# First group's channel attention moved into the last merged turn and the second cross attention, 26 of its expert chunks beside the second half's feed-forward and projections, and seven chunks a turn in place of nine

## The chip, the cores and the metric

The kernel runs on one core of one Trainium2 chip. The metric is the device time of one execution in microseconds; the median of several runs counts. The core's engines are TensorE (PE, with its weight loads PEld), VectorE (DVE), ScalarE (ACT), GpSimd (POOL) and SyncE (SP), which here only issues DMAs. They run their own instruction lists in written order and wait for each other by semaphores.

## The reference, cut to what matters

A decoder with two layers over x of 16 sequences × 128 tokens × 128 channels, in f32. Layer 0: four encoder layers of linear attention with 16 heads and a feed-forward; cross attention against a context with 16 heads and a mask; a feed-forward with quantized weights and activations, in which a depthwise convolution over three tokens stands between the two products. Layer 1:

```python
# self attention with 16 heads of 8, each row keeps its 64 largest scores
# channel attention (_L1_xattn), n = 128 tokens, 4 heads of d = 32 channels, with global and local weights
scores = jnp.einsum('bhdn,bhen->bhde', qh, kh) * scale
attn = jax.nn.softmax(scores, axis=-1)
out = jnp.einsum('bhde,bhen->bhdn', attn, vh)
# mixture of 8 experts, all of them over all tokens (HIDDEN 128, FFN 512)
y = sum over experts of (silu(h @ Wg) * (h @ Wu)) @ Wd
```

Every step has a residual sum, and most have a layer norm in front.

## The kernel before, in words

The 16 sequences are two halves of 8; a half is two slots (s = 0, 1) of G = 4 sequences, and a slot of a half is a group (g = 0 to 3) in layer 1. A tile of a slot is 128 × 512 f32. PSUM has eight banks of 128 × 512.

The program is, on each engine: `encode_half` (half 0 through the encoder), `cross_and_forward(0)`, `beside_encoder` (half 0's topk self attention, sequence by sequence, merged with half 1's encoder: the merged turns, b = −1 to 9), `cross_and_forward(1)`, and then one loop over points `t`. Twelve points are one turn, which belongs to one sequence b of the topk attention: at turn b the signs and penalties of b are worked on, the search for the 64th largest score of b−1, and the probabilities and outputs of b−2. The loop begins at `START2` = 84, turn 7, and the topk part ends with turn 17, at point 216. There is no run-time planner: each engine's order is what these point lists say, and a function `topk(b, p, half)`, `channel(g, r)`, `expert_chunk(k)`, `gate(k)` or `hidden(k)` issues on each engine what belongs to the point.

`channel(g, r)` is the channel attention of group g, r = 0 to 11, from point `CH_START[g]` on: keys with their row weights on GpSimd (r 0 and 2), statistics and normalization (r 1, 2), queries (r 3, 4), 64 small score matmuls (r 5), softmax (r 6, 7), spreading of the weights into blocks on GpSimd (r 7), output matmuls (r 8), residual, statistics and normalization again (r 9, 10), and a transpose into `hTm`, the experts' input (r 11). It goes through PSUM bank 3. It starts at 84 (group 0), 102 (group 1), 166 and 214.

An expert chunk k is one of 4 pieces (128 hidden channels) of one of 8 experts for one group: 32 a group, 128 in all. TensorE makes the gate product into bank 5 or 6 (line 1519), the down product of chunk k−3 into bank 4 (1509), and the up product into bank 3 or 7 (1528); ScalarE applies Silu (1045); VectorE multiplies (2008). `chunk_points` places the chunks: from 12 points behind their group's `CH_START`, at the points `CHUNK_PTS` of a turn (nine of twelve), and behind point 216 at every point. So turns 8 to 17 have nine each, and 38 come in the tail. SyncE loads an expert's three 256 KB weights into one of two buffers when the chunks of the one before last are done.

In `cross_and_forward(hf)`, the core of the cross attention runs eight iterations (one a sequence): scores into banks 0 to 3; on VectorE a masked copy (2277), row maxima (2282), sums of the iteration before (1752), and the folding of heads for the outputs of three iterations back (1761, 1764); exponentials on ScalarE; subtraction and scaling on GpSimd; transposes through banks 4 and 5, outputs (1225) into banks 6 and 7 by turns. Then come the quantized feed-forward, c = 0 to 3 with two slots each, slot 0 in banks 0 to 3 and slot 1 in 4 to 7, the second quantization and product, a layer norm and the projections for the topk attention.

Of the kernel before, what the change touches and what calls it, by code (L numbers as in the profile page):

```python
# [26 lines left out]
P = 128  # L27
NSEQ = 16
SLOTS = 2
G = 4  # L30
# [51 lines left out]
CROSS_BANKS = (((2, 3, 0, 1), (6, 7, 4, 5)), ((3, 4, 5, 5), (6, 7, 4, 5)))  # L82

# [36 lines left out]

def gate_point(t):

    return t + max(0, 2 - t % PTS) if t < TURNS * PTS else t


def hidden_point(t):
    return t if t >= TURNS * PTS else t + 2 if t % PTS < 2 else t + 1
# [28 lines left out]
U_BANK, U_PREV = u_banks()  # L156

# [13 lines left out]
def decoder(nc, x, ctx, mask, aw, acolA, acolB, arow, w2a, bw, bcol, brow, cw, cconv, dw, dcol, drow,  # L171
            erow, ecol, mg, mu, md, ident_d, const_d, pos_d, out):
    stack = ExitStack()
    with stack:
# [142 lines left out]
        def flat(t):  # L317
# [5 lines left out]
                   [t[:, :, :].rearrange("p b c -> p (b c)")[:, 0:2 * P].bitcast(BF16).rearrange("p (i q) -> p i q", i=4) for t in xin]]  # L323
# [4 lines left out]
        hid = [big[1][:, i, :] for i in range(CH)]  # L328
        hp = h[0]
        hTm = [hT[1][:, :], flat(xb[1])]  # L330
        sg = [qe[s][:, :] for s in range(SLOTS)]
        ctxp = ctxt[0]
        ctxTp = cbuf[0][:, :, 1:P + 1]
        ysb = ctxt[1]
        chq, chk = kk, ke
        chv = [xb[0], h[1]]
        ablk = [t[:, :, 0:P] for t in vv]
# [98 lines left out]
        def _(sp):  # L436
# [72 lines left out]
            def load_keys(g):  # L509
                sp.dma_start(ctxp[:, :, :], cv[:, g * G:(g + 1) * G, :]).then_inc(ctxp_in, 16)  # L510

            for l in range(L - 1):
# [10 lines left out]
                load_down(l + 1)  # L523
            sp.wait_ge(at_mm, 2)
# [3 lines left out]
            load_keys(0)  # L528
            for e in range(2, NG * NEXP):
                if e % NEXP == 2 and e // NEXP + 1 < NG:  # L530
# [12 lines left out]
        def _(pool):  # L543
# [35 lines left out]
            def core_cross(hf):  # L579
# [30 lines left out]
                for b in range(1, NB):  # L610
# [5 lines left out]
                    if b + 2 < NB:  # L616
                        spread(b + 2)

# [20 lines left out]
            def spread_queries(b):  # L639
                g, c = b // G, b % G  # L640
                if b >= 2:
                    pool.wait_ge(st_mm, 2 * (b - 2) + 2)
                pool.tensor_tensor(qblk[b % 2],
# [56 lines left out]
            def channel(g, r):  # L700
                x = xs_of[g // SLOTS][g % SLOTS]
                if r == 0:
# [5 lines left out]
                    for k in range(2):  # L708
                        pool.tensor_tensor(chk[k][:, :, :], ctxp[:, :, :], bc(rowe[:, 4 + 2 * k, :]), ALU.mult).then_inc(c_k, 1)
# [9 lines left out]
                if r == 7:  # L719
# [3 lines left out]
                    for k in range(2):  # L723
                        pool.tensor_tensor(ablk[k].rearrange("p a (q e) -> p a q e", q=EH),
# [48 lines left out]
            def beside_encoder():  # L773
# [3 lines left out]
                for b in range(-1, NB + 2):  # L777
                    merged_turn(b)
                    if b == NB:
                        for s in SL:  # L780
                            ln_rsqrt(s, NLN + LN_B)

# [43 lines left out]
            for t in range(START2, LAST_POINT):  # L826
                if t < TURNS * PTS:
                    topk(t // PTS, t % PTS, 1)
                for g in range(NG):
# [3 lines left out]
        def _(act):  # L833
# [29 lines left out]
            def core_cross(hf):  # L863
                for b in range(NB + 2):
                    if 1 <= b <= NB:
                        exponentials_by_head(hf, b - 1)
                    if b >= 2:
                        copy_probs(hf, b - 2)

            def projected(s, hf):  # L870
                qT, kT = qT_of[hf], kT_of[hf]

                hT_copy(s, hf * NTR + TR_D, 4 * s)
                act.wait_ge(pk_mm, nth(s, hf * 2 + 2))
                act.activation(kT[s][:, :], bank(4 * s + 2), ACT.Identity, bias=catt[1][:, 1:2]).then_inc(pk_done, 1)
                act.wait_ge(pq_mm, nth(s, hf * 2 + 2))
                act.activation(qT[s][:, :], bank(4 * s + 1), ACT.Identity, bias=catt[1][:, 0:1]).then_inc(pq_done, 1)
# [8 lines left out]
            def signs(n, heads):  # L886
# [3 lines left out]
                if n >= 2:  # L890
                    act.wait_ge(z_ready, 3 * n - 3)
                for hd in heads:
# [114 lines left out]
            def beside_encoder():  # L1007
                for b in range(-1, NB + 2):
# [3 lines left out]
                    if b == NB + 1:  # L1012
                        context_queries(1)
                        attended_out(1, 6)

            def channel(g, r):
                if r == 0 and g > 1:
                    attended_out(g, 3)
                if r == 2:
                    act.wait_ge(cT_mm, g + 1)  # L1020
                    act.copy(ctxTp, bank4(3)).then_inc(cT_out, 1)
                if r == 3:
# [5 lines left out]
                    if g == 0:  # L1028
                        act.wait_ge(base_done, 4 * HALVES)
                    for k in range(2):  # L1030
                        act.activation(chv[k][:, :, :], ctxTp, ACT.Identity, bias=cole[:, 2 * k + 1:2 * k + 2], scale=cole[:, 2 * k:2 * k + 1]).then_inc(c_v, 1)
# [3 lines left out]
                if r == 11:  # L1035
                    act.wait_ge(m_mm, g + 1)
                    if g >= 2:
                        act.wait_ge(u_mm, NCHUNK * (g - 1))
                    act.copy(hTm[g % 2], bank(3)).then_inc(m_out, 1)  # L1039
# [1443 lines left out]
```

## Time and profile before

| | |
|---|---|
| median of 3 runs | 1509.03 us (1507.82 to 1510.85) |
| the profiled execution, its own time | 1503.95 us |
| its span | 1502.0 us |
| mean granted TensorE clock, share of full | 0.805 |
| busy: PE, PEld | 1055.0, 626.8 us |
| busy: DVE, ACT, POOL | 989.8, 663.2, 484.4 us |
| moved by DMAs | 41.22 MB, mean 27 GB/s |

The page gives busy time per engine, then 40 slices of the span (37.6 us each), in which a digit is the busy share in tenths. The clock row is in tenths of full speed, 2.4 GHz; TensorE is granted 2.4 or 1.2 GHz, and values between are means. Ends of matmuls are modelled, and they overlap, so what one costs is read from the distance of starts. A timeline gives instructions in order of time, with equal neighbours merged, and in square brackets the idle time of the engine before it and what ended it.

### The profile page before, as it was taken

The numbers are of one execution on the slowest core, as the hardware profiler recorded it, in microseconds if no ns is written. First come the engines' busy times: TensorE is split into PE (matmuls) and PEld (weight loads), VectorE is DVE, ScalarE is ACT, GpSimd is POOL, SyncE is SP. The second block draws the span as 40 slices with busy tenths as digits, with TensorE's granted clock in tenths as the row PEclk, the third lists the DMA queues.
The fourth block names the chain that finished last, engine by engine and source line by source line (L and its number), as shares of the span: only waits on it lengthen the run. The fifth ranks groups of instructions, "written<-read, shape, count | busy, mean of one in ns | idle before, by whom it ended". The sixth has DMA issues, their size and how long they took to land. (4 is left out here: it accounts for less than half of the span.)

```text
span 1502.0 us, 16867 instructions
## 1 busy us (share of the span) xinstructions
PE 1055.0 (70%) x4698; PEld 626.8 (42%) x4698; DVE 989.8 (66%) x3078; ACT 663.2 (44%) x1751; POOL 484.4 (32%) x446
## 2 busy tenths in 40 slices
PE   3877745545667277787655545769999487998798
PEld 2766622323445155565433323334444144453333
DVE  6566678887467877775858887376666776644222
ACT  2444427532566255563127433455666255323121
POOL 4233337403345144443227305442222143101000
PEclk9899967855677577775558756799999778999899
DMA  3110010000000000000010000011211001112111
GB/s 120 29 28 19 18 47 1 1 0 1 1 13 17 13 17 13 17 2 1 1 49 1 1 0 8 1 42 43 64 57 43 21 22 42 57 63 63 49 63 49
DMA packets 34124, 41.22 MB, mean 27 GB/s; under 512 B 5280, under 2 KB 19248, under 8 KB 34032
## 3 DMA queue, kind: packets, MB, share of 16 engines
q1 hardware_dynamic: 33360, 38.21, 8.2%
q0 software_dynamic: 672, 1.98, 0.4%
q8 instruction: 34, 0.56, 0.2%
q14 instruction: 58, 0.48, 0.1%
HBM read 39.13 MB, written 1.05 MB: 27 GB/s over the span
## 5 line engine op out<-in xcount | busy, mean ns | idle before, releaser
L2008 DVE TENSOR_TENSOR big<-psum,qe 128x512 f32<-128x512 f32 x128 | 87.7, 687 | 211.6 <-PE psum L1528 103.7
L1045 ACT ACTIVATE qe<-psum 128x512 f32<-128x512 f32 x128 | 75.1, 596 | 199.0 <-PE psum L1519 196.5
L1509 PE MATMUL psum<-big,wexp 128*128 128x512 f32 x256 | 135.3, 612 | 0.0
L903 ACT ACTIVATE far<-far,half_far,fmul 128x128 bf16<-128x128 bf16 x256 | 103.2, 487 | 51.7 <-DVE hit L1786 51.7
L1799 DVE MAX8 near<-Wk 128x8 f32<-128x128 f32 x512 | 103.5, 276 | 1.2 <-DVE Wk L1809 0.2
L572 POOL TENSOR_SCALAR veps<-mv 128x4 f32<-128x4 f32 x34 | 8.3, 246 | 276.2 <-DVE mv L1706 276.2
L1148 PE MATMUL psum<-ident,h 128*128 128x128 f32 x176 | 38.5, 350 | 79.8 <-DVE h L1713 48.0
L661 POOL TENSOR_TENSOR Wk<-Wk,far 128x1024 f32<-128x1024 f32 x32 | 69.2, 2162 | 73.2 <-ACT far L903 73.2
L1284 PE MATMUL psum<-ctxT,kT 32*128 32x512 f32 x128 | 46.2, 802 | 55.5 <-DVEq L1875 42.0
L1528 PE MATMUL psum<-hT,wexp 128*128 128x512 f32 x128 | 70.6, 634 | 20.7 <-DVE big L2008 20.7
L1713 DVE TENSOR_SCALAR h<-xs,mv,rstd 128x128 f32<-128x128 f32 x128 | 56.5, 504 | 41.9 <-POOL rstd L574 38.7
L1214 PE MATMUL psum<-ident,Wk 128*128 128x128 f32 x256 | 47.1, 351 | 45.1 <-POOL Wk L615 41.4
L1519 PE MATMUL psum<-xb,wexp 128*128 128x512 f32 x128 | 72.7, 652 | 8.4 <-DMA wexp<-in_md 7.1
L1509 PEld LDWEIGHTS psum<-big,wexp 128*128 128x128 f32 x256 | 50.7, 198 | 65.1 <-issue 64.9
L1519 PE MATMUL psum<-hT,wexp 128*128 128x512 f32 x128 | 72.8, 652 | 4.6 <-DMA wexp<-in_md 3.6
L893 ACT ACTIVATE far<-S 128x128 bf16<-128x128 f32 x256 | 75.2, 297 | 0.3
L883 ACT ACTIVATE S<-psum,tiny 128x1024 f32<-128x1024 f32 x32 | 35.6, 1114 | 84.6 <-PE psum L1266 84.6
L1528 PE MATMUL psum<-xb,wexp 128*128 128x512 f32 x128 | 67.6, 611 | 6.8 <-DVE big L2008 6.8
L652 POOL TENSOR_TENSOR Wk<-S,ngr 128x2048 f32<-128x2048 f32 x16 | 57.8, 3609 | 44.3 <-DVE hit L1786 44.3
L1809 DVE MATCH_REPLACE8 Wk<-near,Wk 128x128 f32<-128x128 f32 x256 | 67.3, 276 | 0.0
L1148 PEld LDWEIGHTS psum<-ident,h 128*128 128x128 f32 x176 | 25.8, 178 | 95.0 <-DVE h L1713 43.7
L1214 PEld LDWEIGHTS psum<-ident,Wk 128*128 128x128 f32 x256 | 37.4, 180 | 66.2 <-POOL Wk L615 40.5
(320 smaller groups left out, 2705.9 us busy)
## 6 DMA issues: line engine op xcount, KB each, us to landing
wexp<-in_mg SPq DMA_DIRECT2D x32, 256.0 KB, 2.7
wexp<-in_mu SPq DMA_DIRECT2D x32, 256.0 KB, 3.0
wexp<-in_md SPq DMA_DIRECT2D x32, 256.0 KB, 3.5
w<-in_aw SPq DMA_DIRECT2D x8, 256.0 KB, 2.8
w<-in_w2a SPq DMA_DIRECT2D x8, 256.0 KB, 2.6
ctxt<-in_ctx SPq DMA_DIRECT2D x8, 256.0 KB, 4.2
wqkv<-in_aw SPq DMA_DIRECT2D x8, 192.0 KB, 2.2
xin<-in_x SPq DMA_DIRECT2D x4, 256.0 KB, 3.2
```

The lines of the kernel that those rows point to most:

```text
L661: pool.tensor_tensor(Wk[t][:, heads, :], Wk[t][:, heads, :], far[t][:, heads, :], ALU.subtract).then_inc(z_ready, 1)
L893: ins = act.activation(far[n % 2][:, hd, :], S[n % 3][:, hd, :], ACT.Sign, accum_out=cnt[n % 2][:, hd:hd + 1])
L903: ins = act.activation(far[t][:, hd, :], far[t][:, hd, :], ACT.Identity, bias=half_far[:, 0:1], scale=fmul[t][:, hd:hd + 1])
L1045: act.activation(sg[k % 2], bank(5 + k % 2), ACT.Silu).then_inc(silu_done, 1)
L1148: mm = pe.transpose(dst[:, b * P:(b + 1) * P], src[:, b, :], eye)
L1214: mm = pe.transpose(bank(4 + g % 2)[:, j * P:(j + 1) * P], E[a % 2][:, 4 * g + j, :], ident[:, :])
L1509: pe.matmul(bank(4), wd[e % 2][:, c, :], hid[k % CH], start=(k % NCHUNK == 0), stop=(k % NCHUNK == NCHUNK - 1), skip_group_check=True).the ...
L1519: pe.matmul(bank(5 + k % 2), wg[e % 2][:, c * P:(c + 1) * P], hTm[g % 2], start=True, stop=True).then_inc(g_mm, 1)
L1528: pe.matmul(bank(U_BANK[k]), wu[e % 2][:, c * P:(c + 1) * P], hTm[g % 2], start=True, stop=True).then_inc(u_mm, 1)
L1799: ins = dve.max(near[:, hd, rank:rank + 8], Wk[t][:, hd, :])
L1809: ins = dve.match_replace(Wk[t][:, hd, :], near[:, hd, 0:8], Wk[t][:, hd, :], TAKEN)
L2008: dve.tensor_tensor(hid[k % CH], bank(U_BANK[k]), sg[k % 2], ALU.mult).then_inc(hu_done, 1)
```

## The change

Group 0's channel attention and its first 26 expert chunks get points below 84: `FIRST` = 46 is the first. A function `beside(n)` on each engine issues the next n points of them. It is called with 2 points in the last merged turn, with 4, 3 and 3 behind cross-attention iterations 1 to 3 of the second half, and with 26 in the second half's feed-forward and projections: two behind the first product, three in each of the four convolution steps, four around the second product, and four behind each slot's projections. Group 1's channel attention starts at 84 in place of 102. `CHUNK_PTS` has seven points in place of nine, and point 1 of a turn is left out beside a channel attention. To make room, the second half's feed-forward and projections use banks 0 to 3 alone (two a slot), its cross attention's outputs use bank 6 alone, group 0's channel attention and all early up products use bank 7, and several tiles are placed elsewhere.

```diff
-CH_START = (START2, START2 + 18, (2 * G + 5) * PTS + 10 + (G - 4) * PTS, (3 * G + 5) * PTS + 10 + (G - 4) * PTS)
+PRE_TURN, PRE_CROSS, PRE_FORWARD = 2, (4, 3, 3), 26
+FIRST = START2 - PRE_TURN - sum(PRE_CROSS) - PRE_FORWARD
+CH_START = (FIRST, START2, (2 * G + 5) * PTS + 10 + (G - 4) * PTS, (3 * G + 5) * PTS + 10 + (G - 4) * PTS)
-CHUNK_PTS = (0, 1, 3, 4, 5, 6, 7, 9, 10)
+CHUNK_PTS = (0, 1, 3, 4, 6, 7, 9)
...
+OUT_BANKS = ((6, 7), (6, 6))
+FORWARD_BANKS = (((0, 1, 2, 3, 0, 1, 2), (4, 5, 6, 7, 4, 5, 6)), ((0, 1, 0, 1, 0, 1, 0), (2, 3, 2, 3, 2, 3, 2)))
+PROJECT_BANKS = (((0, 2, 1, 3), (4, 6, 5, 7)), ((0, 1, 0, 1), (2, 3, 2, 3)))
+CROSS_OUT_BANKS = ((2, 3), (0, 3))
+X_BANK = (7, 3, 3, 3)
...
-            while t < TURNS * PTS and t % PTS not in CHUNK_PTS:
+            while START2 <= t < TURNS * PTS and (t % PTS not in CHUNK_PTS or t % PTS == 1 and any(c <= t < c + X_FREE for c in CH_START)):
...
-        q = 7 if in_x(t) or k % 2 else 3
+        q = 7 if t < START2 or in_x(t) or k % 2 else 3
...
+            point = [FIRST]
+            def beside(n):                     # TensorE's; the other engines' are alike
+                for _ in range(n):
+                    channel(0, point[0] - CH_START[0])
+                    for k in CHUNKS_OF.get(point[0], ()):
+                        expert_chunk(k)
+                    point[0] += 1
...
@@ TensorE, cross attention: outputs(a) @@
-                    if a >= 2:
+                    if a >= 1 and hf == 1:
+                        pe.wait_ge(o_done, n)
+                    elif a >= 2:
                         pe.wait_ge(o_done, n - 1)
...
@@ TensorE, feed-forward @@
                 first(0)
+                if hf == 1:
+                    beside(2)
                 for c in range(CH):
                     if c + 1 < CH:
                         first(c + 1)
                     for s in SL:
+                        if hf == 1:
+                            beside(1)
                         pe.wait_ge(c_conv, nth(s, hf * CH + c + 1))
...
+                    if hf == 1:
+                        beside(1)
...
                 for s in SL:
                     topk_projections(s, hf)
+                    if hf == 1:
+                        beside(4)
...
@@ SyncE: the first group's context is loaded earlier, the second's with a wait @@
+            sp.wait_ge(q_pos, both(1, 2 * L))
+            load_keys(0)
             sp.wait_ge(at_mm, 2)
             for k in range(2):
                 load_expert(k, k)
             sp.wait_ge(ctxT_mm, nth(1, HALVES))
-            load_keys(0)
+            sp.wait_ge(c_k, 2)
+            sp.wait_ge(cT_mm, 1)
+            load_keys(1)
```

## Rows read from the trace of the kernel before

**Rows 1.** The page: busy time by engine, and 40 slices of PE and of its clock.
```profile
PE 1055.0 (70%) x4698; PEld 626.8 (42%) x4698; DVE 989.8 (66%) x3078; ACT 663.2 (44%) x1751; POOL 484.4 (32%) x446
...
PE   3877745545667277787655545769999487998798
...
PEclk9899967855677577775558756799999778999899
```
**Rows 2.** Windows: length, busy us (x) of PE PEld DVE ACT POOL, clock, DMA share, GB/s.
```profile
769.00:851.00 82.00, 44.09 (x250) 23.22 (x250) 69.64 (x59) 49.90 (x167) 46.18 (x21) 0.73 0.05 17
851.00:872.00 21.00, 8.19 (x38) 3.93 (x38) 14.78 (x52) 2.74 (x6) 2.53 (x4) 0.64 0.00 0
872.00:899.00 27.00, 11.53 (x43) 5.68 (x42) 25.47 (x43) 12.32 (x18) 0.00 (x0) 0.63 0.00 1
899.00:923.00 24.00, 17.32 (x96) 11.40 (x94) 19.70 (x59) 8.22 (x14) 11.64 (x11) 0.67 0.00 0
923.00:951.00 28.00, 9.76 (x97) 6.46 (x97) 15.61 (x44) 11.43 (x41) 10.45 (x12) 0.54 0.04 10
951.00:985.00 34.00, 29.35 (x126) 11.76 (x127) 14.94 (x27) 21.09 (x64) 17.65 (x16) 0.88 0.08 24
985.00:1028.00 43.00, 31.49 (x89) 14.18 (x90) 31.30 (x113) 23.52 (x70) 14.61 (x15) 0.92 0.12 38
...
1068.00:1106.00 38.00, 34.71 (x138) 17.33 (x137) 25.32 (x97) 24.55 (x69) 11.42 (x11) 1.00 0.21 66
1106.00:1143.00 37.00, 35.35 (x126) 16.79 (x126) 24.18 (x94) 23.57 (x67) 11.06 (x10) 0.95 0.14 43
1143.00:1204.00 61.00, 36.07 (x134) 17.78 (x134) 43.02 (x198) 24.39 (x68) 14.42 (x14) 0.84 0.08 26
1204.00:1258.00 54.00, 44.33 (x211) 23.98 (x208) 41.15 (x124) 29.22 (x74) 20.71 (x17) 0.83 0.10 34
1258.00:1303.00 45.00, 36.51 (x124) 18.77 (x121) 26.82 (x104) 17.77 (x35) 11.61 (x11) 0.89 0.18 60
1303.00:1336.00 33.00, 32.04 (x128) 16.14 (x126) 19.30 (x76) 11.47 (x16) 2.04 (x2) 1.00 0.15 48
1336.00:1370.00 34.00, 31.13 (x117) 16.15 (x116) 7.46 (x15) 9.19 (x14) 0.00 (x0) 1.00 0.15 47
1370.00:1401.00 31.00, 20.16 (x121) 9.72 (x120) 16.82 (x39) 8.83 (x13) 8.30 (x9) 0.92 0.16 52
1401.00:1502.00 101.00, 90.74 (x206) 38.67 (x205) 23.41 (x34) 20.28 (x34) 0.00 (x0) 0.97 0.18 60
```
**Rows 3.** Timeline of PE in the tail: start, us, first matmuls of two chunks running.
```profile
1408.79 1.02 PE L1519 MATMUL psum<-xb,wexp 128*128 128x512 f32 x2
...
1411.37 1.02 PE L1519 MATMUL psum<-xb,wexp 128*128 128x512 f32 x2
```
**Rows 4.** The page's groups: busy, mean ns of one; idle before, and releasers.
```profile
L2008 DVE TENSOR_TENSOR big<-psum,qe 128x512 f32<-128x512 f32 x128 | 87.7, 687 | 211.6 <-PE psum L1528 103.7
```
**Rows 5.** Timelines of PE and DVE in two cross-attention iterations, at half and full clock.
```profile
802.25 1.93 PE L1225 MATMUL psum<-big,vv 128*32 128x512 f32 x8 [0.68 <-ACT big L851]
804.11 1.90 PE L1202 MATMUL psum<-kblk,qT 32*128 32x512 f32 x8
...
813.10 1.06 PE L1225 MATMUL psum<-big,vv 128*32 128x512 f32 x8 [0.68 <-ACT big L851]
814.10 1.14 PE L1202 MATMUL psum<-kblk,qT 32*128 32x512 f32 x8
...
815.45 2.47 DVE L2277 COPY_PREDICATED S<-maskt,psum 128x2048 f32<-128x2048 int32 x1 [1.16 <-PE psum L1202]
```
**Rows 6.** Timeline of ACT in turn 12: a table load, the last chunk's gate.
```profile
1115.28 1.28 ACT L1045 ACT_TABLE_LOAD   x1
...
1139.43 0.60 ACT L1045 ACTIVATE qe<-psum 128x512 f32<-128x512 f32 x1 [1.98 <-PE psum L1519]
```
**Rows 7.** Timelines of POOL and DVE in turn 7's channel attention.
```profile
920.44 2.93 POOL L709 TENSOR_TENSOR ke<-ctxt,rowe 128x512 f32<-128x512 f32 x2
...
925.92 3.75 DVE L1940 TENSOR_SCALAR h<-xs,mv,rstd 128x128 f32<-128x128 f32 x4 [1.58 <-POOL rstd L698]
```

More of the change, by code:

```diff
@@ L156 @@
 U_BANK, U_PREV = u_banks()
+EARLY = sum(t < START2 for t in CHUNK_AT)
 def channels_by(t):
@@ L828, in _ @@
                     topk(t // PTS, t % PTS, 1)
-                for g in range(NG):
+                for g in range(1, NG):
                     channel(g, t - CH_START[g])
@@ L891, in signs @@
                     act.wait_ge(z_ready, 3 * n - 3)
+                if n == NB and heads[0] == 0:
+                    act.wait_ge(d_mm, EARLY)
                 for hd in heads:
@@ L1083, in encode_half, with beside @@
                                                bias=colB[:, 2 + c:3 + c]).then_inc(hid_done, 1)
+            point = [FIRST]
+            def beside(n):
+                for _ in range(n):
+                    channel(0, point[0] - CH_START[0])
+                    for k in GATES_OF.get(point[0], ()):
+                        gate(k)
+                    point[0] += 1
             def context_keys(hf):
@@ L1136, in _ @@
                     topk(t // PTS, t % PTS, 1)
-                for g in range(NG):
+                for g in range(1, NG):
                     channel(g, t - CH_START[g])
@@ L1252, in core_cross @@
                         scores(b + 1)
+                    if hf == 1 and 1 <= b <= len(PRE_CROSS):
+                        beside(PRE_CROSS[b - 1])
                 project_outputs(1)
@@ L1655, in cross_and_forward @@
                             pe.wait_ge(c_silu, nth(s, hf * CH + c))
-                        transposes(bank(4 * s + 3), yT[s], ident[:, :], c_yT_mm)
+                        transposes(bank(FORWARD_BANKS[hf][s][3]), yT[s], ident[:, :], c_yT_mm)
+                    if hf == 1:
+                        beside(1)
                 for s in SL:
@@ L1683, in _ @@
                     topk(t // PTS, t % PTS, 1)
-                for g in range(NG):
+                for g in range(1, NG):
                     channel(g, t - CH_START[g])
@@ L2013, in result, with beside @@
                 dve.tensor_tensor(x[:, :, :], bank4(3), x[:, :, :], ALU.add).then_inc(y_done, 1)
+            point = [FIRST]
+            def beside(n):
+                for _ in range(n):
+                    channel(0, point[0] - CH_START[0])
+                    for k in HIDDEN_OF.get(point[0], ()):
+                        hidden(k)
+                    point[0] += 1
             def act_scales(s, n):
@@ L2290, in cross_and_forward @@
                         cross_outputs(hf, b - 3)
+                    if hf == 1 and 1 <= b <= len(PRE_CROSS):
+                        beside(PRE_CROSS[b - 1])
                     if b == NB:
@@ L2325, in cross_and_forward @@
                 quantize(1)
+                if hf == 1:
+                    beside(2)
                 def chunk_max(s, c):
@@ L2409, in _ @@
                     topk(t // PTS, t % PTS, 1)
-                for g in range(NG):
+                for g in range(1, NG):
                     channel(g, t - CH_START[g])
```

175 lines of the change are left out of this document (113 added, 62 removed).

## The prediction

> **What bounds the kernel now.** I read the engines' shares and the 40 slices first. TensorE is busy 70% of the span, VectorE 66%, and neither is busy all the time: TensorE stands mostly at 4 to 7 tenths up to slice 26 and mostly at 8 to 9 from there on [rows 1]. So the second reading is a table of windows, one per stage of the last 730 us [rows 2]. The second half's cross attention is 769 to 851: VectorE 69.6 of 82 us. The convolutional feed-forward and the projections are 851 to 923; from 872 on VectorE works 45 of 51 us and TensorE 28.9 at a granted clock of 0.65. In turn 7 (923 to 951) a chain of small steps, the first group's channel attention, runs over all engines, with TensorE busy 9.8 of 28 us. Turns 8 to 17 (951 to 1370) carry nine expert chunks each, 90 in all, and there TensorE is the bound: in turns 11 and 12 it is busy 34.7 of 38 and 35.4 of 37 us at a clock of 1.00 and 0.95. The tail carries the other 38 chunks in 132 us.
>
> A chunk at full clock costs 2.58 us of TensorE: its first matmul starts at 1408.79, the next chunk's at 1411.37 [rows 3]. It also costs 0.69 us of VectorE (the product, line 2008) [rows 4] and 0.60 us of ScalarE [rows 6]. Turn 13 contains one row set that takes the long way on VectorE: 61 us, with TensorE's work the same as in a turn of 37 [rows 2]. These 24 us depend on the data and stay.
>
> **What the change moves.** By the point lists, chunks per turn were 9 in turns 8 to 17, and 38 in the tail. They become 26 in the feed-forward and projections (points 58 to 83); 6, 6, 7, 7, 7, 5, 0, 0, 6, 7, 7 in turns 7 to 17; and 44 in the tail. Turns 13 and 14 get none, because group 1 is finished at turn 12 and group 2's channel attention is still to come. I price each stretch.
>
> *Last merged turn and cross attention: +20 us (11 to 29).* Group 0's channel attention is now issued on all five engines between the cross-attention iterations. Its VectorE work is what turn 7 shows, 15.6 us [rows 2]; the normalization in it took 3.75 us beside GpSimd work [rows 7], which it will meet again here. GpSimd gets some 10.5 us more in the same place, two of its first steps (2.93 us [rows 7]) and a reciprocal root now stand ahead of the spreads that the first scores wait for, some 2 us. VectorE is the cross attention's bound, with 12.4 us idle in 82, and a part of the added 15.6 falls into its early idle time: I count 12. Second, all outputs of heads now go through one bank (6) instead of two. So TensorE's outputs(a) wait until VectorE has folded a−1, the last thing in VectorE's iteration, and the next scores are queued behind them, for which VectorE waits at its next masked copy. Outputs and scores start 1.0 us apart and take 1.06 and 1.14 at full clock, 1.93 and 1.90 at half [rows 5]: 2.2 to 3.9 us late per iteration, less the idle that is there already (1.16 in the one shown). In iterations 1 to 3 the channel work covers it; three are left: +6 (3 to 9). 2+12+6 = 20.
>
> *Feed-forward and projections: +44 us (34 to 65).* 26 chunks add 26 × 2.58 = 67 us of TensorE, 18 of VectorE and 16 of ScalarE to a stretch of 51 us, so TensorE takes over as the bound. Its own work there is 28.9 us at a clock of 0.65, thus about 18.8 at full clock (an estimate from the windows [rows 2]). 67+18.8 = 86. On top I put 9 for what can't be filled: the first two chunks at half clock with the Silu table load (1.28 us [rows 6]) ahead of VectorE's first product, and the wait for the second quantization. 95 instead of 51. With no such idle it is +35; at a mean clock of 0.8 it is 107+9, +65. Each up-projection there waits for the product of the chunk before (one bank, 7, for all), but VectorE's product stands just ahead of the convolution that TensorE's transposes wait for anyway, so I price that wait at nothing beyond these 9; if the cover is gone it is one VectorE convolution pair, 1.5 us, a chunk. Four chunks stand between the two slots' projections and four behind them: these 20 us are bare, with only 5.8 us of VectorE's topk preparation beside them.
>
> *Turn 7: +7 (2 to 13).* The chain stays (now group 1's), with six chunks beside it. 15.5 us of TensorE mostly fit in its 18 idle us, but six products (4.1 us) enter VectorE's part of the chain, one chunk stands ahead of the score matmuls, and two table loads come in. TensorE's steps of the chain may run at the higher clock, −2.
>
> *Turns 8 to 17: −87 (−103 to −60).* Where TensorE bounds, a chunk less is 2.58 us less. Turn 8: 34 − 3×2.58 = 26. Turn 9 loses two chunks and group 1's channel attention, which made it 43 against turn 12's 37: 32. Turns 10 and 11: 40 and 38 less 5.2, 34 and 33. ScalarE agrees with that: its last signs in turn 12 waited 1.98 us for the gate matmul of the ninth chunk [rows 6], which goes. Turn 12 keeps five chunks, of the late ones none: 31. Turn 13 without chunks: VectorE's own work is 24.2 − 6.2 = 18 us, ScalarE's 23.6 − 5.4 − 2.6 (two table loads) = 15.6 [rows 2, 6], and they hand over to each other; between 18 and the 31 of a five-chunk turn I take 24.5, and 24 for the long way: 48.5. Turn 14: the same with channel attention of group 2, VectorE 18+15: 34 instead of 54. Turn 15: 45−7.7, 36.5 with its idle ends. Turns 16, 17: 28 and 29. Together 332 against 419.
>
> *Tail: +6 (1 to 14).* Six chunks more are 15.5 us, but before, TensorE stood still for 11 of the 31 us around group 3's channel attention [rows 2] for lack of chunks. Now 12 chunks (31 us) and 4.8 us of its steps fill 37. The last 32 chunks stay.
>
> Sum: 20+44+7−87+6 = −10 us. The profiled execution took 1503.95 us around a span of 1502.0, the median of the runs is 1509.03; the same −10 gives 1494 and 1499.
>
> **The clock, weighed against a rule.** The rows show the granted clock at 0.54 where TensorE is busy 35% (turn 7), 0.63 at 43% (872 to 899), and 0.95 to 1.00 above 90% [rows 2]. I price the chunks of the feed-forward at 2.4 GHz, since TensorE has work all the time there. The Trainium skill (TensorE: Matmul & The Clock Gate, Part 1) says that the slow clock is the default and that activity releases it; by this the filled feed-forward is fast, and the emptied turns 13 and 14 are slow. That part speaks against the change, and it is a rival below.
>
> **Rivals.**
> (a) *The forecast*, 1499, own range 1486 to 1512: 0.46.
> (b) *Slower: the filled stages cost more than they free.* Place: points 58 to 83. One bank for the up-projections ties TensorE and VectorE chunk by chunk, and TensorE's clock doesn't stay up: 107+9 and 1 to 2 us more of handing over in 12 convolution chunks make +70 instead of +44, and the sum +16, 1525. It decides from +57 (then the sum is over 3). For it: in 769 to 923 the clock never averages over 0.73. Against: turns 8 to 12 have the same handing over at 0.88 to 1.00. 0.21.
> (c) *The turns are not TensorE's.* If the chain over ScalarE and VectorE ends a turn, seven chunks take 35.5, not 32.5 to 34, and an empty one 30: −62 in place of −87, the sum +15, 1524. For it: ScalarE is busy 23.6 and VectorE 24.2 of turn 12's 37 us, all in written order; against: ScalarE's wait for TensorE [rows 6] and TensorE at 94%. 0.11.
> (d) *Clock in the emptied turns.* TensorE's topk work is 37−9×2.58 = 13.8 us in a turn at full clock, 27.6 at half; turns 13 and 14 then last at least 28 and 38 and turn 15 starts slow: +9, the sum −1, 1508, no change. For it: 0.54 to 0.73 in all five windows from 769 to 951, where TensorE is busy 35 to 72%; against: 0.84 in turn 13 with its 25 idle us. 0.07.
> (e) *More gain*: the cross attention absorbs the channel work (+11), the feed-forward takes +37, empty turns 20: −33, 1476. 0.15.
>
> **Chances and range.** What a measurement of this kernel can tell is about 0.2%, 3 us. Of (a) 0.35 is faster by more, 0.07 within, 0.04 slower; (b) and (c) give 0.26 slower, 0.04 within, 0.02 faster; (d) 0.03, 0.02, 0.02 for faster, within, slower; (e) 0.15 faster; together 0.55, 0.13, 0.32. The bounds of all terms added would reach from −55 to +61, which they won't do together; the range to 1472 and 1532 leaves a tenth on either side.
>
> **What would show it.** Right: the feed-forward at 90 to 100 us with the clock over 0.85; VectorE idle before the masked copy by 2 to 3 us in iterations 5 to 7, ended by TensorE's scores; turns of 32 to 34 us with seven chunks, TensorE over 90% busy; turn 13 near 48, turn 14 near 34; the tail from point 216 near 138. Wrong: a clock of 0.5 to 0.7 between chunks in the feed-forward; turns with seven chunks over 35 us in which TensorE waits for ScalarE; cross attention over 110 us.

## The result: 1.2% slower, and the profile after

| | before | after |
|---|---|---|
| median | 1508.42 us (1497.15 to 1510.85, 4 runs) | 1524.09 us (1521.25 to 1527.53, 4 runs) |
| ratio | | 1.012, 95% interval 1.0065 to 1.0175 |
| the profiled execution, its span | 1503.95, 1502.0 us | 1527.53, 1525.7 us |

The forecast was 1499 us, faster. The time lies inside the range, the sign is wrong. The two spans differ by +23.7 us, where the sum said −10.

The page of the changed kernel, shares and the slices of PE and of its clock, to be held against [rows 1]:

```profile
PE 1077.9 (71%) x4698; PEld 640.8 (42%) x4698; DVE 997.1 (65%) x3078; ACT 653.2 (43%) x1743; POOL 483.2 (32%) x446
...
PE   3878745545767277877836568788899627898998
...
PEclk9989967756687577775557779899999555899999
```

Slices 24 to 27, the filled feed-forward, read 6, 8, 7 and 8 for PE where they read 4, 5, 7 and 6; slices 32 and 33 (turns 13 and 14) read 6 and 2 for PE and 5 for the clock. The windows of the changed kernel, one a stage, columns as in [rows 2]:

```profile
771.50:883.00 111.50, 55.59 (x341) 30.57 (x342) 89.31 (x86) 53.28 (x173) 59.88 (x34) 0.68 0.02 7
...
903.00:947.00 44.00, 41.00 (x119) 18.70 (x117) 32.89 (x55) 20.77 (x32) 0.00 (x0) 0.98 0.11 36
947.00:1001.50 54.50, 43.94 (x156) 21.28 (x156) 25.77 (x70) 14.18 (x24) 11.05 (x11) 0.87 0.14 44
1001.50:1037.00 35.50, 29.54 (x140) 13.30 (x140) 18.98 (x43) 16.19 (x48) 9.29 (x10) 0.90 0.14 45
...
1123.00:1156.50 33.50, 30.14 (x113) 14.62 (x113) 23.43 (x93) 22.56 (x65) 11.36 (x11) 0.95 0.10 34
1156.50:1190.00 33.50, 26.19 (x101) 13.09 (x101) 22.17 (x91) 21.59 (x63) 11.63 (x12) 0.87 0.10 39
1190.00:1242.00 52.00, 23.61 (x90) 14.63 (x90) 39.14 (x192) 19.31 (x64) 14.55 (x15) 0.50 0.00 1
1242.00:1283.00 41.00, 23.25 (x156) 16.61 (x152) 36.31 (x115) 17.78 (x56) 20.42 (x16) 0.50 0.00 1
...
1381.00:1425.50 44.50, 37.62 (x160) 17.66 (x160) 20.81 (x48) 12.61 (x19) 8.30 (x9) 0.96 0.17 54
```

The line 111.50 is the last of the merged turn and the cross attention, 44.00 and 54.50 are the feed-forward and the projections, 35.50 is turn 7, 33.50 twice turns 11 and 12, 52.00 and 41.00 the emptied turns 13 and 14, and 44.50 the twelve chunks around group 3's channel attention. The cut at 1001.5 stands ahead of the last two of the 26 early chunks: turn 7's own first gate product starts at 1006.77, and its channel attention on VectorE at 1007.63. So the stages are measured between instructions that both traces have. For the feed-forward these are the last masked copy and the first statistics of turn 7's channel attention, before and after:

```profile
832.74 2.47 DVE L2277 COPY_PREDICATED S<-maskt,psum 128x2048 f32<-128x2048 int32 x1 [1.30 <-PE psum L1202]
...
922.96 0.85 DVE L1929 BATCH_NORM_STATS2 stats<-xs 128x6 f32<-128x128 f32 x4
```
```profile
864.64 2.46 DVE L2385 COPY_PREDICATED S<-maskt,psum 128x2048 f32<-128x2048 int32 x1 [4.04 <-PE psum L1279]
...
1007.63 0.86 DVE L2026 BATCH_NORM_STATS2 stats<-xs 128x6 f32<-128x128 f32 x4
```

The later bounds are the first gate products of turn 8, of the tail and of group 3's chunks.

| stage | said | measured |
|---|---|---|
| last merged turn and cross attention, to its last masked copy | +20 | +32 (107.1 for 75.5) |
| feed-forward and projections, with all 26 chunks | +44 | +53 (143.0 for 90.2 us) |
| turn 7 | +7 | +3 (31.2 for 28.0) |
| turns 8 to 17 | −87 | −76 (342.5 for 418.7) |
| the tail | +6 | +13 (44.2 for 31.1 beside channel attention, −1 behind it) |

### The profile page after: what moved, and what is told of

Same layout as the page of the kernel before. It is cut to its first block, busy times and chain, and to the rows that moved or that the text cites. A ratio compares the mean times of both kernels' runs of the same rounds, so it can differ in the third digit from the quotient of the medians.

```text
span 1525.7 us, 16858 instructions
## 1 busy us (share of the span) xinstructions
PE 1077.9 (71%) x4698; PEld 640.8 (42%) x4698; DVE 997.1 (65%) x3078; ACT 653.2 (43%) x1743; POOL 483.2 (32%) x446
## 4 chain that ended last, share of the span: by engine, by line
PE 41%; DVE 23%; ACT 7%; issue 5%; POOL 5%; DMA 3%; DVEq 1%; SPq 1%; POOLq 0%; ACTq 0%
PE psum L1601 6%; PE psum L1591 5%; PE psum L1610 5%; PE psum L1389 4%; DMA wexp<-in_md 3%; PE psum L1365 2%; PE psum L1347 2%; ACT far L951 2%; PE psum L1478 2%; PE psum L1485 2%; DVE nmax L1978 2%; DVE S L2385 2%; DVE smax L2390 2%; PE psum L1435 2%; PE psum L1214 1%
## 5 line engine op out<-in xcount | busy, mean ns | idle before, releaser
L2106 DVE TENSOR_TENSOR big<-psum,qe 128x512 f32<-128x512 f32 x102 | 70.1, 688 | 189.6 <-PE psum L1610 98.7
L1092 ACT ACTIVATE qe<-psum 128x512 f32<-128x512 f32 x102 | 59.8, 595 | 160.9 <-PE psum L1601 160.8
L1591 PE MATMUL psum<-big,wexp 128*128 128x512 f32 x204 | 110.3, 625 | 0.0
L1365 PE MATMUL psum<-ctxT,kT 32*128 32x512 f32 x128 | 51.3, 886 | 50.8 <-DVEq L1972 42.8
L1601 PE MATMUL psum<-xin,wexp 128*128 128x512 f32 x128 | 75.2, 671 | 5.7 <-ACT qe L1092 3.4
L1610 PE MATMUL psum<-xin,wexp 128*128 128x512 f32 x128 | 69.9, 629 | 9.9 <-DVE far L2106 6.4
L1591 PEld LDWEIGHTS psum<-big,wexp 128*128 128x128 f32 x204 | 41.2, 202 | 53.6 <-issue 52.9
L902 ACT ACTIVATE Wk<-S,nsm 128x128 f32<-128x128 f32 x128 | 49.5, 389 | 29.1 <-DVE nsm L2392 29.1
L895 ACT COPY big<-psum 128x512 f32<-128x512 f32 x64 | 35.8, 586 | 48.8 <-PE psum L1291 48.5
```

What stands on the lines that cost most here:

```text
L1365: pe.matmul(bank(j), kT_of[g // 2][g % 2][rows, c * P:(c + 1) * P], qblk[a % 2][rows, :, :].rearrange("p i q -> p (i q)"), start=True, sto ...
L1591: pe.matmul(bank(4), wd[e % 2][:, c, :], hid_of[k >= EARLY][k % CH], start=(k % NCHUNK == 0), stop=(k % NCHUNK == NCHUNK - 1), skip_group_ ...
L1601: pe.matmul(bank(5 + k % 2), wg[e % 2][:, c * P:(c + 1) * P], hTm[g], start=True, stop=True).then_inc(g_mm, 1)
L1610: pe.matmul(bank(U_BANK[k]), wu[e % 2][:, c * P:(c + 1) * P], hTm[g], start=True, stop=True).then_inc(u_mm, 1)
L2106: dve.tensor_tensor(hid_of[k >= EARLY][k % CH], bank(U_BANK[k]), sg_of[k >= EARLY][k % 2], ALU.mult).then_inc(hu_done, 1)
```

## The cross attention, read closely

VectorE's channel work in iteration 1 of the changed kernel, first VectorE, then GpSimd, timelines as in [rows 5]:

```profile
789.62 6.52 DVE L2037 TENSOR_SCALAR qe<-xs,mv,rstd 128x128 f32<-128x128 f32 x4
796.25 3.24 DVE L2070 TENSOR_TENSOR kk<-qe,rowe 128x512 f32<-128x512 f32 x2
799.42 1.28 DVE L2074 TENSOR_TENSOR kk<-kk,rowe 128x512 f32<-128x512 f32 x2
800.62 2.44 DVE L2385 COPY_PREDICATED S<-maskt,psum 128x2048 f32<-128x2048 int32 x1
...
808.91 2.50 DVE L2087 TENSOR_TENSOR se<-se,sm 128x256 f32<-128x256 f32 x1
...
825.85 1.11 DVE L2037 TENSOR_SCALAR qe<-xs,mv,rstd 128x128 f32<-128x128 f32 x4 [1.58 <-POOL rstd L740]
```
```profile
790.23 3.61 POOL L646 TENSOR_TENSOR Wk<-Wk,zden 128x2048 f32<-128x2048 f32 x1
793.80 1.04 POOL L622 TENSOR_TENSOR kblk<-kT,consts 128x512 f32<-128x512 f32 x1
794.79 2.48 POOL L757 TENSOR_TENSOR ke<-ke,rowe 128x512 f32<-128x512 f32 x2
...
807.53 3.61 POOL L646 TENSOR_TENSOR Wk<-Wk,zden 128x2048 f32<-128x2048 f32 x1
```

Four normalizations of one form take 1.11 us at 825.85, where GpSimd is idle, and 6.52 at 789.62, beside GpSimd's scaling of the probabilities and the two operations behind it. At 808.91 the product takes 2.50 us and ends at 811.41; GpSimd's operation ends at 811.14. VectorE hardly moved while GpSimd's operation ran. All channel work of VectorE between iterations 1 and 4 adds up to 23 us (11.1, 5.0 and 7.2, its waits inside included), of which 4.6 fell into idle time. The prediction had added the idle-free duration of turn 7, with the one contended row, 3.75 us [rows 7], already inside, and taken off 3.6.

The Trainium skill (SBUF — State Buffer, "Who interferes with whom") says that the port pair which VectorE and GpSimd share is an exclusive lock, not a split of bandwidth; by this rule the loser waits for the whole instruction. The trace agrees at 808.91, to within the 0.27 us by which the product ends later than GpSimd's operation; with GpSimd idle the same product took 0.42 us in turn 7 of the kernel before. On its sentence that a VectorE instruction with one SBUF input outside the 2-port modes doesn't contend, the 6.52 us say only that this normalization isn't in that class.

The one output bank, ahead of the seventh masked copy of the changed kernel, VectorE and TensorE:

```profile
847.25 1.04 DVE L1859 TENSOR_REDUCE hT<-far 128x128 f32<-128x512 f32 x1
852.60 2.45 DVE L2385 COPY_PREDICATED S<-maskt,psum 128x2048 f32<-128x2048 int32 x1 [4.31 <-PE psum L1279]
```
```profile
848.43 1.94 PE L1304 MATMUL psum<-big,vv 128*32 128x512 f32 x8 [5.92 <-DVE hT L1859]
850.30 2.09 PE L1279 MATMUL psum<-kblk,qT 32*128 32x512 f32 x8
```

It is the chain as forecast: fold, outputs, scores, masked copy, at half clock, 1.94 and 2.09 us in a row. TensorE has stood idle for 5.92 us until the fold is done, and VectorE then for 4.31 us until the scores are. The sixth and the eighth copy wait 4.31 and some 4.0 us in the same way, by the profile; run 1 will show that the sixth has another reason.

## The experiments

All ratios are to the kernel before, run on the same chips. The changed kernel stands at 1.012.

**1. Two output banks again.** Bank 7 is the channel attention's up to its transpose, so only from iteration 2 on.

```diff
-OUT_BANKS = ((6, 7), (6, 6))
+OUT_BANKS = ((6, 7) * 4, (6, 6) + (7, 6) * 3)
@@ TensorE, outputs(a) @@
-                    if a >= 1 and hf == 1:
+                    if a == 1 and hf == 1:
                         pe.wait_ge(o_done, n)
                     elif a >= 2:
                         pe.wait_ge(o_done, n - 1)
+                    if a == 2 and hf == 1:
+                        pe.wait_ge(m_out, 1)
```

> The changed kernel (1524), but in the second half's cross attention the outputs go through banks 7 and 6 by turns from iteration 2 on; the first two still take bank 6, since bank 7 is the channel attention's until then. My theory: of the 23.7 us by which the changed kernel's profile is longer, about 11 are the one output bank: VectorE waited 4.3, 4.3 and 4.0 us for TensorE's scores in iterations 4 to 6 where it had waited some 1 us. So 8 to 11 us less, 1513 to 1516, and these waits back at about 1 us. Rival, the whole stretch is bound by the channel work and the shared port of VectorE and GpSimd: then the wait only changes its name, 0 to 3 us less, 1521 to 1524.

Measured: 1516.33 us, 1.005 (1.0025 to 1.0075). TensorE's timeline of this kernel ahead of the sixth copy, and VectorE's with the sixth and seventh:

```profile
838.08 1.94 PE L1306 MATMUL psum<-big,vv 128*32 128x512 f32 x8 [0.68 <-ACT big L895]
839.94 2.09 PE L1279 MATMUL psum<-kblk,qT 32*128 32x512 f32 x8
```
```profile
842.24 2.46 DVE L2387 COPY_PREDICATED S<-maskt,psum 128x2048 f32<-128x2048 int32 x1 [4.17 <-PE psum L1279]
...
850.17 2.43 DVE L2387 COPY_PREDICATED S<-maskt,psum 128x2048 f32<-128x2048 int32 x1
```

The seventh copy doesn't wait any more, and the eighth waits 1.11 us for 4.04. The sixth still does, and its outputs waited for ScalarE's copy of the transposed exponentials, not for the fold: ScalarE's chain had started late, behind the channel work. (In the changed kernel that copy and the fold end within 0.1 us of each other, so taking one away brought nothing there.) From the last step of the merged turn to the last copy it is 99.7 us instead of 107.1. So the theory stands for two of the three waits, 7.4 us of the 11; the third belongs to the channel work. By the ratios the edit brought 10 us, with intervals of some 8 on the changed kernel and 4 on this one; the time is just above the expected range.

**2. The channel attention's first points ahead of the merged turn's end.** VectorE and GpSimd issue r 0 to 4 of group 0 there; the numbers of the counted steps follow.

```diff
@@ VectorE @@
+                beside(5)
                 attended_added(1, 7)
-                beside(PRE_TURN)
@@ GpSimd @@
-                        beside(PRE_TURN)
+                        beside(5)
@@ both, behind iterations 1 to 3 @@
-                        beside(PRE_CROSS[b - 1])
+                        beside((1, 3, 3)[b - 1])
```

> The changed kernel, but VectorE's and GpSimd's first five points of group 0's channel attention stand ahead of the last merged turn's end (where VectorE was idle for 11.5 us), and only 1, 3 and 3 points are left behind the cross attention's iterations 1 to 3. My theory: the 23 us of channel work that VectorE had inside the cross attention (12 were counted) are so many because it met GpSimd's work there, and 2.4 us stood ahead of the first scores; moved forward, about 10 us of it fall into idle time: 8 to 13 us less, 1511 to 1516. Rival, the last merged turn is a chain in itself and only gets longer by what it takes in: 0 to 3 us less, 1521 to 1524.

Measured: 1510.36 us, 1.0023 (0.9998 to 1.0048). The stretch was 96.7 us long instead of 107.1. The rival falls. The single bank's waits are still there, 4.31 us ahead of each of the last three copies; copy to copy, from the fourth to the eighth, it took 15.1, 13.4, 12.3 and 12.3 us.

**3. The kernel before with one output bank.** Nothing else changed.

```diff
-                    if a >= 2:
+                    if a >= 1 and hf == 1:
+                        pe.wait_ge(o_done, n)
+                    elif a >= 2:
                         pe.wait_ge(o_done, n - 1)
...
-bank(6 + a % 2)
+bank(6 + a % 2 * (hf == 0))
```

> The kernel before (1508), with nothing changed but that the second half's cross attention sends all outputs of heads through bank 6. It is the price of one bank by itself. My theory: in iterations 4 to 6 of the changed kernel it was 3.7 us each; here no channel work covers iterations 1 to 3, so five or six iterations pay: 12 to 22 us more, 1520 to 1530. The prediction's 2 to 3 us in three iterations would make 6 to 15 us of five or six, 1514 to 1523. Rival (the bank costs nothing and channel work costs all): 1508 to 1511.

Measured: 1526.19 us, 1.0146 (1.009 to 1.0202). By itself this edit costs about as much as the whole change by the medians; in its trace the stretch from the first to the last copy is 14.6 us longer. VectorE's timeline of this kernel, against 1.16 us of idle in [rows 5]:

```profile
812.56 2.45 DVE L2279 COPY_PREDICATED S<-maskt,psum 128x2048 f32<-128x2048 int32 x1 [4.31 <-PE psum L1202]
```

Four copy-to-copy times in a row are 12.32, 12.32, 12.33 and 12.05 us, where before they are 7.95, 9.22, 7.94 and 9.35. The rival of a free bank falls. In the changed kernel channel work covered all but two of these iterations, so the bank cost 7 there.

**4. Five chunks a turn up to turn 14.** Turns 7 to 14 have 5, 5, 5, 5, 5, 5, 5, 3.

```diff
+THIN_PTS = (0, 3, 4, 6, 9)
-... (t % PTS not in CHUNK_PTS or
+... (t % PTS not in (THIN_PTS if t < 15 * PTS else CHUNK_PTS) or
```

> The changed kernel, but five expert chunks a turn in turns 7 to 14, at points 0, 3, 4, 6 and 9, in place of seven, so that turns 13 and 14 have chunks as well; the chunks are as many, only their places differ. In the changed kernel, turns 13 and 14 lost 18 chunks and got shorter by only some 22 us, 1.2 us for a chunk and not 2.58. My theory: an empty turn is bound by VectorE and ScalarE, and a chunk there is nearly free, while a chunk less in turns 9 to 12 gives back near 2.5 us: 8 to 20 us less in turns 8 to 12, 8 to 15 more in 13 and 14, sum 3 to 8 us less, 1516 to 1521. Rival, ScalarE and VectorE in written order bound the turns of seven chunks too (rival c of the prediction), so that fewer chunks there bring little: 0 to 6 us more, 1524 to 1530. Rival, the clock in the emptied turns (d): at least 9 us less, 1515 or under, with the granted clock near 0.85 in turns 13 and 14.

Measured: 1522.66 us, 1.0102 (1.0065 to 1.0138). By the time alone nothing is settled, the interval overlaps that of the changed kernel. Turn by turn, turns 9 to 14 took 25.5, 30.1, 33.2, 32.0, 57.4 and 41.5 us, and in the changed kernel 28.0, 32.7, 33.4, 33.5, 51.9 and 41.3. Two chunks less in a turn of seven (9 to 11) gave 2.5, 2.6 and 0.2 us, which is 1.3, 1.3 and 0.1 a chunk and not 2.58, so in these two traces TensorE is only a part of what bounds a turn below seven chunks; three more in turn 14 cost 0.2; five more in turn 13 cost 5.5. The 8 to 20 us for turns 8 to 12 were too much, they gave 7.6. Rival d's 9 us didn't come.

**5. Both repairs.** The diffs of 1 and 2 together.

> Both repairs of the cross attention in one kernel: two output banks from iteration 2 on, and the channel attention's first five points ahead of the last merged turn's end. My theory, that these two hold all the cross attention's excess: each took away its own piece (8 and 14 us), and in the second one the wait for the single bank moved into all of iterations 3 to 7, so the two add up: 20 to 24 us under the changed kernel's 1524, ratio to the kernel before 0.990 to 0.998 (1493 to 1503). Rival, they overlap and only one of them counts: ratio 1.001 to 1.004, 1508 to 1512.

Measured: 1505.42 us, 0.9997 (0.9967 to 1.0027): no change against the kernel before. Less than expected. The pieces did add up in the traces (107.1 to 88.8 us, 18.2 off for 7.4 and 10.3), but I had read 14 us off the second one's median, part of which was not the edit's (last section). 13.4 of the 31.6 us stay: the channel work left behind iterations 1 to 3, with the late ScalarE behind it (VectorE's sixth copy waits 3.78 us here), and 1.9 in the last iteration.

**6 and 7. Ten and eighteen chunks in the feed-forward.** Both with the repairs; the calls run out of points early, and the last 16 or 8 early chunks go on to turns 12 to 14.

```diff
-PRE_TURN, PRE_CROSS, PRE_FORWARD = 2, (4, 3, 3), 26
+PRE_TURN, PRE_CROSS, PRE_FORWARD = 2, (4, 3, 3), 10
@@ beside(n), all four engines @@
-                for _ in range(n):
+                for _ in range(min(n, START2 - point[0])):
```

> The kernel with both repairs, but only 10 chunks in the feed-forward (26 before), all of them in its first three convolution steps, and the 16 others in turns 12 (2), 13 (7), 14 (6) and one in the tail. My theory: a chunk in the feed-forward costs 1.8 us, in turns 13 and 14, which VectorE and ScalarE bound, at most 1.2: 8 to 20 us less than the kernel with both repairs. Rival, the prediction's own price (2.58 us a chunk where TensorE bounds, and so in turns 12 to 14 too; 44 us for 26 in the feed-forward): 16 x 1.7 = 27 less and 16 x 2.58 = 41 more, 10 to 15 us more.

> The same with 18 chunks in the feed-forward: eight more of them go to turns 12 (2) and 13 (6), turn 14 stays empty. My theory: 4 to 10 us less than the kernel with both repairs, and the feed-forward with the projections some 14 us shorter. Rival (the prediction's own prices): 3 to 8 us more.

Measured: 1479.87 us with ten, 0.983 (0.9789 to 0.9871), and 1498.04 us with eighteen, 0.9949 (0.992 to 0.9978). The kernel with ten beats both. The windows of the kernels with 26 (run 5), 18 and 10, in that order: from the last masked copy to turn 8, then turns 8 to 11, turn 12, turn 13, turn 14, and the rest (of the kernel with 18 the first two alone).

```profile
848.10:1022.80 174.70, 132.62 (x516) 64.69 (x517) 108.23 (x234) 63.92 (x136) 28.34 (x27) 0.87 0.10 32
1022.80:1141.50 118.70, 105.23 (x329) 47.13 (x327) 77.56 (x291) 80.41 (x249) 42.87 (x36) 0.93 0.15 48
1141.50:1174.90 33.40, 26.08 (x101) 13.00 (x101) 22.05 (x91) 21.69 (x63) 11.68 (x12) 0.87 0.11 37
1174.90:1226.80 51.90, 23.62 (x90) 14.61 (x90) 39.16 (x193) 19.23 (x62) 14.40 (x15) 0.50 0.00 1
1226.80:1268.00 41.20, 23.23 (x156) 16.61 (x152) 36.28 (x115) 18.01 (x57) 20.65 (x16) 0.50 0.00 1
1268.00:1508.10 240.10, 212.07 (x688) 99.69 (x688) 93.67 (x268) 66.64 (x111) 22.54 (x24) 0.95 0.17 54
```
```profile
839.60:987.50 147.90, 107.11 (x466) 53.41 (x468) 102.81 (x227) 58.96 (x128) 28.33 (x27) 0.87 0.09 27
987.50:1111.90 124.40, 108.76 (x331) 48.41 (x329) 77.29 (x290) 80.48 (x249) 42.85 (x35) 0.90 0.14 46
```
```profile
848.20:980.40 132.20, 90.42 (x421) 47.72 (x423) 99.14 (x219) 54.26 (x120) 29.29 (x27) 0.82 0.06 18
980.40:1100.80 120.40, 103.60 (x329) 46.78 (x327) 77.41 (x291) 80.39 (x249) 42.85 (x36) 0.94 0.16 47
1100.80:1135.20 34.40, 31.20 (x113) 15.12 (x113) 23.25 (x93) 22.59 (x65) 11.23 (x11) 0.90 0.12 37
1135.20:1194.40 59.20, 34.89 (x132) 17.59 (x132) 42.40 (x200) 24.30 (x70) 14.93 (x16) 0.76 0.09 27
1194.40:1238.80 44.40, 34.56 (x192) 19.86 (x188) 39.65 (x122) 26.48 (x67) 18.88 (x17) 0.78 0.09 27
1238.80:1478.70 239.90, 211.04 (x694) 98.40 (x694) 94.50 (x269) 68.61 (x112) 22.50 (x23) 0.96 0.17 56
```

The last 8 of 26 chunks cost (174.7 − 147.9)/8 = 3.35 us each, the 8 before them (147.9 − 132.2)/8 = 1.96. Taken only up to the first statistics of turn 7's channel attention, the stretch is 144.6, 118.9 and 103.7 us, and 90.2 in the kernel before: 3.2 and 1.9 each, and 1.3 for each of the first ten. In turns 12, 13 and 14 the chunks put back cost 1.0 for 2, 7.3 for 7 and 3.2 for 6, that is 0.77 each. The change had taken them from where they were cheap and put the last of them where they were dearest. Turns 8 to 11, the same work in all three kernels, read 118.7, 124.4 and 120.4 us, so some us of each difference belong to the one execution: the step between 3.35 and 1.96 is less certain than the 2.66 that all 16 cost, (174.7 − 132.2)/16. From the last masked copy to the end, the traces with 18 and ten are 13.3 and 29.5 us shorter than that with 26; the medians of the whole differ by 7.4 and 25.6, with intervals of 4 to 6 on each. Of the measured gains, 26 us is over what I expected and 7 inside, since the last ones in the feed-forward cost more than the mean of 1.8 that I had used.

**8. TensorE kept busy in the emptied turns.**

```diff
+                if 13 * PTS <= t < 15 * PTS and t % PTS in CHUNK_PTS:
+                    pe.wait_ge(silu_done, 64)
+                    for _ in range(2):
+                        pe.matmul(bank(5), ident[:, :], rowe[:, 0:4, :]..., start=True, stop=True)
```

> The changed kernel (1524), with two extra 128x512 f32 products into bank 5 at seven points of each of the emptied turns 13 and 14. Nobody reads them; they are 14 x 2 products, 28 us of TensorE at half clock or 14 at full, and they only keep it busier. It tells why the emptied turns stayed long (51.9 and 41.3 us). Rival d of the prediction, the granted clock of 0.50 makes them long: the clock rises above 0.7 there and turns 13 and 14 get 5 us or more shorter in spite of the added work. My theory, VectorE's and ScalarE's own chain is the length: the clock may rise, and the two turns stay within 3 us of what they were, the total 1521 to 1528.

Measured: 1524.41 us, 1.0115 (1.0081 to 1.015). The windows of turns 13 and 14 of this kernel:

```profile
1183.00:1234.10 51.10, 30.21 (x118) 15.73 (x118) 39.53 (x193) 19.12 (x62) 14.37 (x15) 0.76 0.00 1
1234.10:1277.20 43.10, 31.71 (x180) 18.01 (x176) 36.27 (x114) 17.98 (x57) 20.38 (x15) 0.70 0.00 1
```

The clock went from 0.50 to 0.76 and 0.70, and the turns from 51.9 and 41.3 us to 51.1 and 43.1. The low clock was there, as rival d had it, and what it cost was little: all that VectorE waited directly for TensorE in the two turns is 7.8 us in the changed kernel (6.1 and 1.7) and 9.0 here (5.0 and 4.0), where the added products also stand in TensorE's list. That bounds the clock's part at some 8 of the 93 us. VectorE's work, the same in either kernel, is the larger part of both turns, 39.5 and 36.3 us. The Trainium skill (TensorE: Matmul & The Clock Gate, Part 1) says that activity releases the throttle of the clock; the clock in these rows agrees with that, while the length of the turns hardly moved.

**9. Ten chunks, without the repairs.** The same edit as 6 on the changed kernel.

> The changed kernel with that one number altered: 10 chunks in the feed-forward instead of 26, none of the repairs of the cross attention. With both repairs this step brought 26 us. My theory, that the last 16 chunks of the feed-forward are the one large error (they cost 3 us each there and under 1 in turns 12 to 14) and that it has nothing to do with the cross attention: 22 to 29 us less than the changed kernel, ratio to the kernel before 0.990 to 0.998, so faster by this alone. Rival, the step brings so much only behind a cross attention without its stalls: 10 to 18 less, ratio 1.000 to 1.006.

Measured: 1495.53 us, 0.993 (0.9905 to 0.9956). So one number turns the change from 1.2% slower into 0.7% faster.

**10. Six chunks in the feed-forward, nine points in turns 13 and 14.** Run 6 with

```diff
-PRE_TURN, PRE_CROSS, PRE_FORWARD = 2, (4, 3, 3), 10
+PRE_TURN, PRE_CROSS, PRE_FORWARD = 2, (4, 3, 3), 6
+THIN_PTS = (0, 1, 3, 4, 5, 6, 7, 9, 10)
-... (t % PTS not in CHUNK_PTS or
+... (t % PTS not in (THIN_PTS if 13 * PTS <= t < 15 * PTS else CHUNK_PTS) or
```

> Both repairs, six chunks in the feed-forward instead of ten; turns 13 and 14 take nine and eight instead of seven and six. In the feed-forward the first ten chunks cost 1.3 us each, in turns 13 and 14 the thirteen cost 0.8 each. My theory, both prices rise with the number, and the two are near each other here: within 5 us of the kernel with ten chunks, ratio 0.980 to 0.986. Rival, TensorE bounds turns 13 and 14 once they are full: 2.58 us each, 5 us or more longer, ratio 0.986 or above.

Measured: 1482.22 us, 0.9832 (0.9798 to 0.9866), as good as ten. The stretch to turn 8 was 127.0 us (132.2), turn 13 63.7 (59.2), turn 14 48.0 (44.4). These 5.2 off and 8.1 on, for four chunks each way, have the two places equal or the feed-forward still the cheaper one for the last few.

**11. Four chunks and nine a turn.** Run 6 with

```diff
-PRE_TURN, PRE_CROSS, PRE_FORWARD = 2, (4, 3, 3), 10
+PRE_TURN, PRE_CROSS, PRE_FORWARD = 2, (4, 3, 3), 4
-CHUNK_PTS = (0, 1, 3, 4, 6, 7, 9)
+CHUNK_PTS = (0, 1, 3, 4, 5, 6, 7, 9, 10)
```

> Both repairs, four chunks in the feed-forward, and nine chunks a turn as in the kernel before (8, 8, 9, 9, 9, 9, 8, 1, 8, 9, 9 in turns 7 to 17, 37 in the tail). It tells what the early channel attention alone brings, and what seven a turn bring. My theory: nine chunks in a turn cost over 2 us each above seven, while turn 14 stays empty, so this is 3 to 12 us longer than the kernel with ten and seven, ratio 0.985 to 0.992. Rival, the number in a turn doesn't matter while the sum is the same: ratio 0.980 to 0.984.

Measured: 1493.96 us, 0.9906 (0.9871 to 0.994). Turns 10 to 12 took 39.2, 38.9 and 37.1 us, with seven chunks 33.4, 33.3 and 34.4 in the trace of run 6: 2.3 us a chunk there. So above seven chunks TensorE does bound those turns.

**12. The changed kernel with nine points.**

```diff
-CHUNK_PTS = (0, 1, 3, 4, 6, 7, 9)
+CHUNK_PTS = (0, 1, 3, 4, 5, 6, 7, 9, 10)
```

> The changed kernel with nine points for chunks in a turn instead of seven, nothing else: 6, 8, 9, 9, 6 chunks in turns 7 to 11, none in 12 and 13, one in 14, 8, 9, 9 in turns 15 to 17, 37 in the tail instead of 44. It isolates that edit. My theory: turns 9 and 10 cost 4.5 us more each for two chunks, turn 12 saves only 2 to 5 for its five, turns 15 to 17 and the tail exchange six or seven chunks at 2.6 us each: 0 to 8 us more than the changed kernel, 1524 to 1532. Rival, the empty turns are worth as much as TensorE's work in them: 1520 to 1524.

Measured: 1530.86 us, 1.0178 (1.0136 to 1.0219). The intervals of this kernel and of the changed one (1.0065 to 1.0175) overlap. With run 11, seven a turn looks like the right half of the change, but that isn't shown by the times.

## Why the prediction was wrong

The sum was −10 us, the traces differ by +23.7. The misses are 12 us in the cross attention, 11 in turns 8 to 17, 9 in the feed-forward and 6 in the tail, with 4 the other way in turn 7.

*Turns 8 to 17*, −87, measured −76, is the step that failed by its reasoning: "an empty turn" was priced from turn 12's engines. For turns 8 to 11 the pricing by TensorE held or was too high: 24.6, 28.0, 32.7 and 33.4 us for 26, 32, 34 and 33. It failed where TensorE was no longer the bound. Turn 12 with five chunks took 33.5 for 31. Turn 14 was put at 34, from 18 us of VectorE in turn 12 plus 15 for the channel attention; but turn 14's own row has 41.15 us of VectorE, and less nine products of 0.69 [rows 2, 4] that is 35.0, more than the forecast of the whole turn. It had 36.3 and took 41.3. Turn 13's row gives 36.8 in the same way; it took 51.9 for 48.5. Turns 12 to 14 together are 13 us over, turns 15 to 17 some 4, which no run looks into. This is rival c's mechanism, in turns 12 to 14 and, by the trace of run 4, perhaps wherever a turn has fewer than seven chunks; run 8 leaves rival d a few us at most.

*The cross attention*, +20, was mis-sized by 12 us. The bank's part, 7.4 for 6 (run 1), came out near by two errors against each other: 3.7 us in each of two iterations, where some 2 in each of three had been counted. The channel work and what stands ahead of the first scores cost 24 for 14: VectorE had 23 us of it, because GpSimd's long operations held it, and ScalarE's exponentials came late behind it for one iteration more, which I hadn't counted. Ten of the 24 could be had back by issuing its first points where VectorE stands idle, in the merged turn (run 2); GpSimd works beside them there too, and the four normalizations took 3.02 us.

*The feed-forward*, +44, measured +53, was right in its cause and mis-sized: TensorE was busy 41 of 44 us at a clock of 0.98 in the convolution steps. From 903 to 1007.6 it was busy 91.0 of 104.6 us, for 86 of 95 in the sum. The largest single piece of its idle time is 6.2 us for VectorE's product ahead of an up-projection, the wait that the sum had priced at nothing beyond its 9 us:

```profile
970.60 2.07 PE L1610 MATMUL psum<-xin,wexp 128*128 128x512 f32 x2 [6.19 <-DVE far L2106]
```

Rival b, whose 1525 is nearly the measured time, needed +57 and a low clock between the chunks, and had the wrong mechanism: that its time fits is chance. What the sum didn't ask either is how the cost spreads over the 26 chunks: 1.3 each for ten, 1.9 to 3.4 for the rest (runs 6, 7). Ten chunks in this stretch make the same change faster by 0.7% (run 9).

*Turn 7* took +3 for +7. *The tail* took +12 for +6 (+13 beside the channel attention, −1 behind it): I had counted 12 chunks and 4.8 us of steps as filling it. TensorE still stood 2.49 us for GpSimd ahead of the output matmuls, as in the kernel before, 1.64 for the product and 1.4 in two waits for expert weights (0.39 and 1.0); this stretch wasn't experimented on.

So the errors nearly all went the same way, under a sum of −10. The 0.32 for slower was too low for that: the +44 stood below the middle of its own range (49.5) and the −87 beyond that of its (−81.5), both on the favourable side. That the time lies inside the stated range is owed to the range's width of 60 us.

## What to carry to other kernels

When work is moved, price the marginal unit at both ends, not the mean: the first ten chunks cost 1.3 us each in their new place and the last eight over 3, while one missed in a turn bound by another engine gave back 0.8. Check each forecast stage against the busy time of every engine in that stage's own row; no stage can be shorter than it. And a double buffer taken away to make room is an edit with a price of its own: here, alone, it cost 1.5% (0.9 to 2.0).

## What the runs showed of the hardware

The clock's level at a given place is not the same in each trace, and it moves the time. In the kernel of run 2, 32 down-projection matmuls of the last merged turn took 3.82 us at a granted clock of 1.00; in the kernel before 6.06 at 0.61, with the same work in front. First the kernel before, then that of run 2:

```profile
702.14 3.43 PE L1308 MATMUL psum<-vaug,wexp 128*128 128x10 f32 x16
705.41 6.06 PE L1404 MATMUL psum<-w,big 128*128 128x128 f32 x32
```
```profile
701.31 3.82 PE L1485 MATMUL psum<-w,big 128*128 128x128 f32 x32
```

VectorE waited 15.0 us for them in the one and 6.9 in the other. Turn 11, with seven chunks and the same work, took 43.9 us at a clock of 0.81 in the trace of run 10 and 33.3 at 0.95 in that of run 6; the first is also the slowest execution of its kernel, 1490.45 us against a median of 1482.22. Such places are, I think, most of the 10 to 15 us by which executions of one kernel differ here; this was not measured by itself. So a stage is compared from a bound inside the trace, and a total only over many runs.
